# Walking pixel-major buffers in runs of pixels, and a third of the odd turns' normalisation on VectorE: a fused conv and MoE block on one Trainium2 core

## The reference: what is computed

```
m = mean over channels of x[b, :, p];  v = variance over channels
xn[b, c, p] = (x[b, c, p] - m) / sqrt(v + 1e-6)
```

```
k1 = conv1d(xn over channels, se_key_w[pixel]) + se_key_b[pixel]
x1 = x + alpha * out1 + (1 - alpha) * out2
out = x1 + sum over the token's 2 experts of prob * expert(layernorm(token))
```

## Time and profile before

| | us |
|---|---|
| median of 3 runs | 1658.89 (1657.28 to 1659.47) |
| the profiled execution's own time | 1662.11 |
| its span | 1660.4 |
| PE busy | 1251.2 (75%) |
| DVE busy | 1101.1 (66%) |
| ACT busy | 720.6 (43%) |
| POOL busy | 535.8 (32%) |
| share of the chain that ended last: PE, DVE, ACT, POOL, DMA | 59%, 11%, 8%, 4%, 8% |

### The profile page before, as it was taken

How to read it: one execution, slowest core, us unless ns; L and a number is a source line. 1 busy time by engine, 2 the same in 40 slices (tenths; PEclk the granted TensorE clock), 3 DMA queues, 4 the chain that set the end, 5 groups by cost and what they waited for, 6 DMA issues and landing times.

```text
span 1660.4 us, 36623 instructions
## 1 busy us (share of the span) xinstructions
PE 1251.2 (75%) x9504; PEld 1024.6 (62%) x9505; DVE 1101.1 (66%) x2637; ACT 720.6 (43%) x1741; POOL 535.8 (32%) x497
## 2 busy tenths in 40 slices
PE   0197879896999999997556522999999999999200
PEld 0187778892565565557545512888888888888100
DVE  7796456564778777775676672666666666666493
ACT  0293233333555555554667641333333333333350
POOL 0163111110111111110467774444454545544100
PEclk9997788887999999995555555999999999999655
DMA  8536787869878888861233444222222333222576
GB/s 314 136 91 183 243 285 282 323 240 244 192 175 184 182 185 197 197 147 53 96 131 134 140 155 130 86 86 89 89 89 84 88 92 93 90 90 70 230 284 256
DMA packets 239768, 267.87 MB, mean 161 GB/s; under 512 B 119696, under 2 KB 211988, under 8 KB 235818
## 3 DMA queue, kind: packets, MB, share of 16 engines
q1 hardware_dynamic: 219413, 214.20, 44.6%
q0 software_dynamic: 20320, 53.28, 9.6%
HBM read 158.69 MB, written 116.19 MB: 166 GB/s over the span
## 4 chain that ended last, share of the span: by engine, by line
PE 59%; DVE 11%; ACT 8%; DMA 8%; SPq 4%; issue 4%; POOL 4%; DVEq 0%; POOLq 0%; ACTq 0%
PE ps L803 15%; PE ps L788 14%; POOL rows_d L1621 4%; PE ps L596 3%; PE ps L613 3%; PE ps L562 3%; DMA u_d<-in_zstrings 3%; PE ps L627 2%; PE ps L772 2%; DVE big L1361 2%; PE ps L674 2%; PE ps L629 2%; DVE pool_ L1353 2%; PE ps L618 2%; ACT aux L1493 2%
## 5 line engine op out<-in xcount | busy, mean ns | idle before, releaser
L1630 POOL DMA_INDIRECT y_d<-pool_,to_s x176 | 254.8, 1448 | 278.7 <-DVE pool_ L1321 242.5
L803 PE MATMUL ps<-pool_,aux 128*128 x2112 | 248.7, 274 | 6.0 <-DVE aux L1313 3.4
L788 PE MATMUL ps<-aux,pool_ 128*128 128x256 f16 x2112 | 247.5, 274 | 0.6 <-ACT aux L1543 0.3
L803 PEld LDWEIGHTS ps<-pool_,aux 128*128 128x128 f16 x2112 | 199.8, 98 | 49.9 <-issue 25.3
L788 PEld LDWEIGHTS ps<-aux,pool_ 128*128 x2112 | 206.4, 98 | 25.9 <-issue 1.2
L1543 ACT ACTIVATE aux<-ps,b_s 128x256 f32<-128x256 f32 x352 | 138.3, 475 | 162.5 <-DVE aux L1313 162.0
L1621 POOL DMA_INDIRECT rows_d<-aux,idx_s x162 | 159.0, 982 | 103.4 <-DVE idx_s L1223 54.3
L1610 POOL DMA_DIRECT2D pool_<-v_d x64 | 47.9, 753 | 338.6 <-PE ps L682 323.8
L1321 DVE SCALAR_TENSOR_TENSOR pool_<-ps,pool_ 128x512 f32<-128x512 f32 x88 | 60.9, 692 | 140.6 <-PE ps L803 140.6
L1535 ACT ACTIVATE aux<-ps 128x512 f16<-128x512 f32 x88 | 52.5, 597 | 188.8 <-PE ps L772 188.8
L1313 DVE TENSOR_TENSOR aux<-aux 128x1024 f16<-128x1024 f32 x88 | 107.9, 1226 | 3.1
(11 more groups left out here) (209 smaller groups left out, 2691.2 us busy)
## 6 DMA issues: line engine op xcount, KB each, us to landing
pool_<-rows_d SPq DMA_DIRECT2D x88, 258.0 KB
pool_<-y_d SPq DMA_DIRECT2D x18, 1152.0 KB, 8.5
big<-in_x SPq DMA_DIRECT2D x2, 5184.0 KB, 21.0
xn_d<-big SPq DMA_DIRECT2D x16, 648.0 KB, 5.4
aux<-in_x SPq DMA_DIRECT2D x64, 162.0 KB, 2.9
v_d<-aux SPq DMA_DIRECT2D x64, 162.0 KB, 2.6
ks_d<-big SPq DMA_DIRECT2D x16, 648.0 KB, 3.8
pool_<-v_d POOLq DMA_DIRECT2D x64, 162.0 KB, 3.3
```

The source lines that it names most:

```text
L788: last = nc.tensor.matmul(o, w_s[:, a, bass.ds(e * (4 * PIECE) + (k * HID + j * 128), 128)], xh_s[:, par, b, k * SLOTS:(k + 1) * SLOTS], s ...
L803: last = nc.tensor.matmul(ps[:, 6 + par, s * C:(s + 1) * C], hh_s[:, par, a, j, s * 128:(s + 1) * 128], w_s[:, b, bass.ds(e * (4 * PIECE) ...
L1630: nc.gpsimd.indirect_dma_start(out=y_d[:, :], out_offset=bass.IndirectOffsetOnAxis(ap=to_s[:, par, k:k + 1], axis=0), in_=yo_s[:, par, k, ...
```

## The change

1. Every copy between the layouts keeps the same values but walks them in another order: for each channel its two or three pixels, instead of for each pixel its 256 channels. In `big` and `pool_` these are runs of 2 or 3 neighbours. The other side of each copy is then read or written with a step: PSUM in `k1_out` and `rows`; `xp_s` (1 KB apart) in `xn_back`; `xs_s` (512 bytes apart) in `tokens`; `got_s` (1 KB apart) in `finish`. `normalise` and the one-pixel half of `k1_out` keep their steps.
2. On odd turns (13 of the 27) ACT normalises two pixels, and DVE the third with one tensor_scalar from `big` into `xp_s`. DVE does it for turn 2i+3 between `transposed(2i+1)` and `k1_out(2i)`; turn 1's stands ahead of the loop. A new semaphore `xl_c` tells PE and POOL of it on odd turns. The last pair of turns is taken out of the DVE's loop.

```
-                for k in range(0, PIX, 2):
-                    ins = nc.vector.tensor_tensor(by_pixel(pool_)[:, bass.ds(i * PIX + k, n), :],
-                                                  ps[:, 4 + 2 * par + k // 2, 0:n * C].rearrange("p (k c) -> p k c", k=n),
-                                                  kb_s[:, bass.ds(i * PIX + k, n)].unsqueeze(2).to_broadcast([128, n, C]),
+                    ins = nc.vector.tensor_tensor(pool_.rearrange("b (c p) -> b c p", p=HW)[:, :, bass.ds(i * PIX + k, n)],
+                                                  ps[:, 4 + 2 * par + k // 2, 0:n * C].rearrange("p (k c) -> p c k", k=n),
+                                                  kb_s[:, bass.ds(i * PIX + k, n)].unsqueeze(1).to_broadcast([128, C, n]),
...
+            def last_pixel(i):
+                at = bass.ds(i * PIX + PIX - 1, 1)
+                dve.wait_ge(S["xb_c"], i - 1 + CREDIT)
+                dve.sem_inc(S["settle_v"], 1)
+                nc.vector.tensor_scalar(xp_s[:, 1, PIX - 1:PIX, :], by_pixel(big)[:, at, :], stats[:, 1, at],
+                                        stats[:, 2, at], ALU.mult, ALU.add).then_inc(S["xl_c"], 1)
+            def pixel_turns(i, more=True):
+                transposed(i * 2 + 1, 1)
+                if more:
+                    last_pixel(i * 2 + 3)
+                k1_out(i * 2, 0)
+                transposed(i * 2 + 2, 0)
+                k1_out(i * 2 + 1, 1)
...
-                x1 = x1_turned[:, r * SUBS:(r + 1) * SUBS, :]
+                x1 = x1_turned[:, r * SUBS:(r + 1) * SUBS, :].rearrange("b s c -> b c s")
-                nc.vector.tensor_tensor(x1, x1, got_s[:, slot, 0, at:at + SUBS, :], ALU.add).then_inc(S["fin_c"], 1)
+                nc.vector.tensor_tensor(x1, x1, got_s[:, slot, 0, at:at + SUBS, :].rearrange("b s c -> b c s"),
+                                        ALU.add).then_inc(S["fin_c"], 1)
...
-                for k in range(PIX):
+                for k in range(PIX - par):
...
-                nc.scalar.activation(xs_s[r % 3].rearrange("p h (s b) -> p h s b", s=SUBS),
-                                     x1_pixels[:, :, r * SUBS:(r + 1) * SUBS, :], ACT.Copy).then_inc(S["xs_c"], 1)
+                nc.scalar.activation(xs_s[r % 3].rearrange("p h (s b) -> p h b s", s=SUBS),
+                                     x1_pixels[:, :, :, r * SUBS:(r + 1) * SUBS], ACT.Copy).then_inc(S["xs_c"], 1)
...
-                nc.scalar.activation(x1_turned[:, r * SUBS:(r + 1) * SUBS, :],
+                nc.scalar.activation(x1_turned[:, r * SUBS:(r + 1) * SUBS, :].rearrange("b s c -> b c s"),
-                                     .rearrange("p (s c) -> p s c", s=SUBS), ACT.Copy).then_inc(S["x1t_c"], 1)
+                                     .rearrange("p (s c) -> p c s", s=SUBS), ACT.Copy).then_inc(S["x1t_c"], 1)
...
-            def xn_back(i, par):
+            def xn_back(i, par, odd=0):
                 pool.wait_ge(S["xp_c"], i + 1)
                 settle()
-                nc.gpsimd.tensor_copy(by_pixel(big)[:, bass.ds(i * PIX, PIX), :], xp_s[:, par]).then_inc(S["xb_c"], 1)
+                if par:
+                    pool.wait_ge(S["xl_c"], odd + 1)
+                    settle()
+                nc.gpsimd.tensor_copy(big.rearrange("b (c p) -> b c p", p=HW)[:, :, bass.ds(i * PIX, PIX)],
+                                      xp_s[:, par].rearrange("b k c -> b c k")).then_inc(S["xb_c"], 1)
```

More of the change, by code:

```diff
@@ L261, in metaformer_kernel @@
                    k1_out0 k1_outm kp_out0 kp_out1 ks_out r_out0 r_out1 xr_in0 xr_in1 xr_in2 xr_in3 ra_c r_c
-                   kr_in0 kr_in1 kr_in2 kr_in3 kr_out0 kr_out1 kr_out2 kr_out3 u_in0 u_in1 xp_c xb_c tr_c xt_c k1_c k1_ev tab_in mask_in tab_c xq_c r_in0
+                   kr_in0 kr_in1 kr_in2 kr_in3 kr_out0 kr_out1 kr_out2 kr_out3 u_in0 u_in1 xp_c xl_c xb_c tr_c xt_c k1_c k1_ev tab_in mask_in tab_c xq_c r_in0
                    r_in1 mb_p mb_e0 mb_e1 tq_p pt_c cv_p v_c ks_c st_v0 st_v1 st_v2 st_v3 ch_d kq_in0
@@ L274, in metaformer_kernel @@
         x1_s = big[:, :].rearrange("p (h t) -> p h t", h=HALVES)
-        x1_pixels = big[:, :].rearrange("p (h b n) -> p h n b", h=HALVES, b=BS)
+        x1_pixels = big[:, :].rearrange("p (h b n) -> p h b n", h=HALVES, b=BS)
         x1_turned = by_pixel(big)
@@ L519, in _, with turn_pixels @@
             pe.wait_ge(S["w_in"], W_IN)
-            def turn_pixels(i, par):
+            def turn_pixels(i, par, odd=0):
                 pe.wait_ge(S["xp_c"], i + 1)
+                if par:
+                    pe.wait_ge(S["xl_c"], odd + 1)
                 pe.wait_ge(S["xt_c"], i - 1 + CREDIT)
@@ L548, in _ @@
                 for par in range(2):
-                    turn_pixels(i * 2 + par + 1, 1 - par)
+                    turn_pixels(i * 2 + par + 1, 1 - par, i)
                     convolve_pixels(i * 2 + par, par, i + 1)
@@ L913, in k1_out @@
                     n = min(2, PIX - k)
-                    ins = nc.vector.tensor_tensor(by_pixel(pool_)[:, bass.ds(i * PIX + k, n), :],
-                                                  ps[:, 4 + 2 * par + k // 2, 0:n * C].rearrange("p (k c) -> p k c", k=n),
-                                                  kb_s[:, bass.ds(i * PIX + k, n)].unsqueeze(2).to_broadcast([128, n, C]),
+                    ins = nc.vector.tensor_tensor(pool_.rearrange("b (c p) -> b c p", p=HW)[:, :, bass.ds(i * PIX + k, n)],
+                                                  ps[:, 4 + 2 * par + k // 2, 0:n * C].rearrange("p (k c) -> p c k", k=n),
+                                                  kb_s[:, bass.ds(i * PIX + k, n)].unsqueeze(1).to_broadcast([128, C, n]),
                                                   ALU.add)
                 ins.then_inc(S["k1_ev"], 1)
+            def last_pixel(i):
[11 more added lines that the diff above has]
+                k1_out(i * 2 + 1, 1)
+            dve.wait_ge(S["norm"], 1)
+            last_pixel(1)
             transposed(0, 0)
-            with dve.Fori(0, PIX_TURNS // 2) as i:
-                for par in range(2):
-                    transposed(i * 2 + par + 1, 1 - par)
-                    k1_out(i * 2 + par, par)
+            with dve.Fori(0, PIX_TURNS // 2 - 1) as i:
+                pixel_turns(i)
+            pixel_turns(PIX_TURNS // 2 - 1, more=False)
             k1_out(PIX_TURNS - 1, 0)
@@ L1578, in settle @@
                 pool.sem_inc(S["settle_g"], 1)
-            def xn_back(i, par):
+            def xn_back(i, par, odd=0):
                 pool.wait_ge(S["xp_c"], i + 1)
                 settle()
-                nc.gpsimd.tensor_copy(by_pixel(big)[:, bass.ds(i * PIX, PIX), :], xp_s[:, par]).then_inc(S["xb_c"], 1)
+                if par:
+                    pool.wait_ge(S["xl_c"], odd + 1)
+                    settle()
+                nc.gpsimd.tensor_copy(big.rearrange("b (c p) -> b c p", p=HW)[:, :, bass.ds(i * PIX, PIX)],
+                                      xp_s[:, par].rearrange("b k c -> b c k")).then_inc(S["xb_c"], 1)
             with pool.Fori(0, PIX_TURNS // 2) as i:
                 for par in range(2):
-                    xn_back(i * 2 + par, par)
+                    xn_back(i * 2 + par, par, i)
             xn_back(PIX_TURNS - 1, 0)
```

## The result

| us | before | after |
|---|---|---|
| median of the runs | 1658.85 (1657.28 to 1659.47) | 1644.86 (1642.3 to 1648.03, 4 runs) |
| ratio to before | | 0.9918 (95%: 0.9896 to 0.994) |
| the profiled execution's own time | 1662.11 | 1648.03 |
| its span | 1660.4 | 1646.2 |
| PE, DVE, ACT, POOL busy | 1251.2, 1101.1, 720.6, 535.8 | 1251.0, 1086.3, 694.3, 526.7 |

The change gives 14.0 us, where the forecast had 5.5. The time lies inside the range (1637 to 1665), but near its first rival (1641) and not near the forecast (1653.4): `finish` became cheaper.

A forecast was written before the change was run, and what follows sets the result against it. Pixel convolution bound by PE, the load ring, DVE and ACT nearly equally, scatter by POOL, end by DVE. 1662.11 - 1.0 (pixel convolution) - 4.5 (scatter) - 0 (end) = 1656.6 profiled; median 3.2 lower, 1653.4 us; range 1637 to 1665.

The forecast's parts named there:

- first rival: End stage: `finish` gains too, 0.45 us a turn, if steps over three dense rows are cheap; 1641 us, chance 0.28.
- The end, "0": End stage: `finish` keeps its 1512 ns because its SBUF read stays scattered; gain 0, bounds -15.3 us to no loss.
- `tokens`, "0": Scatter: ACT's `tokens` keeps its 1563 ns because its SBUF write stays scattered; gain 0.
- Runs as good as dense: `k1_out` and `rows`: runs of two or three cost about the dense price, 720 ns on DVE, 850 on ACT.
- The twentieth on top: Allowance added to the dense price for runs: 685 to 720 ns on DVE, 810 to 850 on ACT.
- The scatter, "-4.5": Scatter: seven ACT copies back before POOL's third wait ends, each 0.68 us shorter; -4.5 us, bounds 0 to -5.0.
- The pixel convolution, "-1.0": Pixel convolution: ACT and DVE relieved, but PE and the loads keep the pace; -1.0 us, bounds 0 to -2.
- the ring: Pixel convolution: banded-matrix load, the turn's convolution, next load of the same slot; 2.32 us a turn, forbidding most gain.
- PE's 2.20 us a turn: Pixel convolution: what PE alone was said to need each turn, with nothing but matmuls between transposes.
- DVE's new instruction: Rival, pixel convolution: DVE's tensor_scalar waits for POOL's copy over SBUF; +11 us at three quarters, 1665 us, chance 0.17.
- POOL's copy: Rival, pixel convolution: POOL's 1.56 us copy grows past its 0.71 us of cover; 1657 us, chance 0.09.

The follow-up runs named there:

- e4: The changed kernel with 57 copies added to time single walks on DVE, ACT and POOL; DVE reads of three streams took 1.03 us, dense 0.95.
- e3: The changed kernel with `finish`, `rows` and `tokens` put back as before, leaving the pixel convolution's change alone: 1659.9 us, ratio 0.9996 to the kernel before.
- e9: The changed kernel without 25 of the 27 loads of banded matrices: 1643.64 us in one run, against 1661.36 for the kernel before.
- e11: The changed kernel with each load of banded matrices split in two, the first pixel's issued earlier: 1638.57 us, ratio 0.989 to the kernel before.

## Why the prediction was right in sign and wrong in size

The forecast was 5.5 us and came from the scatter and the pixel convolution; the measured 14.0 came almost all from the end, which it had at nothing. That the time lies inside the range is owed to the first rival, which set the range's lower end, and not to the sum.

1. **The end, "0": the step that failed.** The prediction said "By the rows one scattered side is enough to set the pace, so these three keep their price: 1512, 1563 and 1556 ns". Measured: 1028, 1556 and 1081. The rule came from rows that read or wrote with a step of 324 bytes, each value on a new place and no return to it. A walk round three dense rows is something else, and e4 shows that reads of it cost DVE little more than dense ones. The prediction knew that no row showed this case and kept it as its first rival, at 0.28; its 0.45 us a turn was 0.48. Of the reasons it gave for that rival, a cheap walk over three dense rows is borne out; distance is no part of it: 1 KB and 1040 bytes cost the same.
2. **`tokens`, "0": right, for a reason that did not hold.** It stayed because its scattered side is a write, not because any scattered side sets the pace.
3. **Runs as good as dense: right.** 710 ns for twos (said: 720), 946 for threes on ACT (said: 850). The twentieth on top was too little for ACT: e4 has 0.98 for runs of three against 0.84 dense, a sixth.
4. **The scatter, "-4.5": the lead came, most of it was given back.** Seven copies became 0.59 us shorter, not 0.68, and against the stage's start the third wait ends 3.4 us sooner with all of the change, 3.2 with `rows` alone. What the prediction left out is that POOL's issues are not of a fixed length: from that wait on they took 3.7 us more, and the last issue came 0.3 us later against the stage's start. Of `rows` alone 1.2 us reached the last issue.
5. **The pixel convolution, "-1.0": within its bounds of 0 to -2, too small to be measured, and the ring was rightly named.** The two profiles differ by 0.9 in this stage, but executions with the same code in it differ by 0.8 to 1.3, and e3 shows no gain. That the ring forbids more is shown by e9 and e11. My own doubt of it after the result, read from a chain that shows only PE, was wrong (e9). But PE's 2.20 us a turn was misread: some of it is waiting, PE's matmuls alone are 2.0, and with the ring relieved a turn takes 2.11. So the ring hid 4 us, where the prediction saw 1.7 at most.
6. **The rivals on the other side.** DVE's new instruction did not wait for POOL (0.17 was given to it), and POOL's copy became shorter instead of longer: it now writes runs of three, and three dense streams read with a step of 1 KB cost little (1081 ns).
7. **The sum.** By the profiled executions: up to the first `tokens` -2.9 (0.9 of it in the pixel stage, the rest where the change touches nothing), scatter +0.3, from its last issue to the first load of results +1.1 (1015.36 to 1552.44 against 1017.92 to 1553.95, where the change touches nothing either), end -12.7: together the -14.2 by which the span fell. Outside the end that is -1.5 where the forecast had -5.5.

## What to carry to other kernels

Price each side of a strided copy by how it moves, not by its step: here runs of two and three are near dense both ways, a read that goes round three dense rows is too, and a write that does so isn't; where one side must go round a few rows, let it be the read. A lead on an engine that feeds a queue is worth what is left at the queue's last issue, so compare that one, not the first. Where several resources end within a tenth of a microsecond of each other, a chain that names only the busiest is no proof; take one of the others away.

## What the runs showed of the hardware that I had not expected

- Reads of three interleaved dense streams: 1.03 us for 768 values on DVE against 0.95 dense, and 1.47 for writes; DVE, ACT and POOL are alike in this within 0.06 us.
- An indirect DMA issue on POOL, 0.96 us, lasts up to 1.44 when it begins while DVE runs a two-input instruction with an fp16 result.
- A two-input addition on POOL beside the two-input instructions of DVE: the two take turns, so that an addition takes 3.10 us, or 6.55 where DVE came first once more, and each costs DVE some 2.2 us.
